# Sums of two pairs of node tiles per layer gathered by GpSimd with adding indirect DMAs, in a graph layer and expert kernel

## What is computed

```python
norm = dis[src] * dis[dst]                       # dis = 1/sqrt(degree), self loops included
for l in range(2):
    x_res = x
    h = x @ W[l]
    agg = segment_sum(norm[:, None] * h[src], dst) + b[l]
    x = relu(agg + x_res @ resW + resb)
...
h1 = relu(features @ expert_w1 + b1); h2 = relu(h1 @ expert_w2 + b2); out = h2 @ expert_w3 + b3
combined = sum over the two best experts of weight * out
```

## Time and profile before

| | us |
|---|---|
| three runs, median (lowest to highest) | 2029.84 (2025.51 to 2032.26) |
| the profiled execution, its own time | 2028.8 |
| its span in the trace | 2027.2 |

### The profile page before, as it was taken

One profiled execution on the slowest core, in us unless ns is written; L12 is line 12 of the kernel. 1 busy time (PEld: TensorE's weight loads), 2 busy tenths in 40 slices (PEclk: granted clock), 3 DMA queues, 4 the chain that ended last, 5 costly groups with the idle time before them and its releaser, 6 DMA issues. The chain is left out here.

```text
span 2027.2 us, 34554 instructions
## 1 busy us (share of the span) xinstructions
PE 1845.7 (91%) x11170; PEld 1128.0 (56%) x11170; DVE 1120.7 (55%) x2788; ACT 771.5 (38%) x1686; POOL 387.4 (19%) x403
## 2 busy tenths in 40 slices
PE   4448799999999999999959999999999988998886
PEld 3336555555555555555524445444454476886775
DVE  7246766666666666666504444444444566644443
ACT  2226755665566655665501222222222232221221
POOL 1680000000000000000000211111211133335664
PEclk8769899999999999999979999999999999998998
DMA  6255399998999972323364555444555556767783
GB/s 221 58 85 111 106 330 308 285 333 257 293 293 272 282 248 94 153 108 134 154 274 159 184 193 203 173 174 170 184 202 196 186 183 200 253 214 234 256 254 123
DMA packets 121920, 412.55 MB, mean 204 GB/s; under 512 B 14633, under 2 KB 75009, under 8 KB 115577
## 3 DMA queue, kind: packets, MB, share of 16 engines
q1 hardware_dynamic: 82936, 283.65, 40.2%
q0 software_dynamic: 37904, 124.85, 21.9%
q10 hardware_dynamic: 1008, 3.21, 0.4%
HBM read 201.60 MB, written 219.99 MB: 208 GB/s over the span
## 5 line engine op out<-in xcount | busy, mean ns | idle before, releaser
L1383 PE MATMUL bank<-parts,counts 128*128 128x512 f16 x2401 | 643.3, 378 | 0.0
L1383 PE MATMUL bank<-parts,counts_again 128*128 128x512 f16 x2401 | 540.3, 381 | 18.5 <-DMA counts_again<-counts_table 18.5
L1547 ACT ACTIVATE counts<-bank 128x392 f16<-128x392 f32 x800 | 395.1, 497 | 311.2 <-PE bank L1463 304.5
L1383 PEld LDWEIGHTS bank<-parts,counts_again 128*128 128x128 f16 x2401 | 234.1, 99 | 288.4 <-issue 17.0
L594 DVE TENSOR_TENSOR rows_lo<-pair_keys,iota_lo 128x2048 bf16<-128x2048 bf16 x200 | 244.9, 1225 | 239.4 <-PE bank L1463 239.3
L1463 PEld LDWEIGHTS bank<-rows_hi,rows_lo 128*128 128x128 bf16 x3200 | 227.6, 99 | 203.7 <-issue 27.1
L1463 PE MATMUL bank<-rows_hi,rows_lo 128*128 128x98 bf16 x3200 | 277.8, 210 | 11.3 <-DVE rows_hi L594 10.5
L1383 PEld LDWEIGHTS bank<-parts,counts 128*128 128x128 f16 x2401 | 192.5, 96 | 103.6 <-issue 1.1
L454 POOL DMA_INDIRECT first_rows<-route_rows,route_spot_i x49 | 47.9, 977 | 825.7 <-DVE tokens L445 817.7
L594 DVE TENSOR_TENSOR rows_hi<-pair_keys,iota_hi 128x1568 bf16<-128x1568 bf16 x200 | 193.5, 967 | 0.0
L2261 DVE TENSOR_SCALAR h_t<-bank,counts_again 128x256 f32<-128x256 f32 x120 | 57.7, 483 | 161.4 <-PE bank L2097 115.6
(11 more groups left out here) (259 smaller groups left out, 1843.1 us busy)
## 6 DMA issues: line engine op xcount, KB each, us to landing
counts_table<-counts SPq DMA_DIRECT2D x25, 3136.0 KB, 13.7
counts_again<-counts_table SPq DMA_DIRECT2D x24, 3136.0 KB, 11.4
counts_again<-expert_pack SPq DMA_DIRECT2D x60, 898.0 KB
first_rows<-zero_rows POOLq DMA_DIRECT2D x3, 10530.0 KB, 58.4
second_rows<-zero_rows POOLq DMA_DIRECT2D x3, 10449.0 KB, 70.2
res_tile<-res_table SPq DMA_DIRECT2D x98, 128.0 KB, 6.5
first_rows<-zero_rows POOLq DMA_DIRECT2D x1, 10270.0 KB, 61.8
second_rows<-zero_rows POOLq DMA_DIRECT2D x1, 10191.0 KB, 66.7
```

The lines of the kernel that those rows point to most:

```text
L1383: mm = nc.tensor.matmul(acc[:, 0:2 * dim], lhs, rhs, start=s == 0, stop=s == tiles)
L1547: nc.scalar.activation(counts[:, b, :, :].rearrange("p s (o n) -> p o s n", o=2)[:, :, :, q * QUAD:(q + 1) * QUAD], bank[4 + q % 4][:, 0:Q ...
```

## The change

1. **Gathered sums.** Pairs 18 and 20 (`GATHERED`) no longer have counts. A float32 copy of all messages is kept in DRAM for each layer (`message_table`). The sum of each of their four tiles is made by GpSimd: in round n an indirect DMA reads, for each of the 128 nodes of a tile, the message of its n-th edge's source and adds it (`compute_op=ALU.add`) to `gathered_sums`. Nodes have up to 56 edges (`RUN`), shorter lists point at rows of zeros. So there are 56 rounds of four DMAs (128 rows of 1 KB each), 224 in each layer. The two DMAs of a pair wait until that pair's round before has landed. In layer 0 the 56 rounds stand one behind the other in GpSimd's queue; in layer 1 there are 8 rounds first, and then 3 behind the scatters of each pair.
2. **PE, DVE, ACT** do 23 pairs in both layers. The work that follows a sum (transposes, products, routing) stays for all 49 tiles; for pairs 18 and 20 it is put beside the pair after. In layer 1 the order of the routing of the pairs 17 to 23 is written out by hand (`LATE_ROUTES`), with a third buffer and a second bank.
3. **Preparation.** GpSimd's 40 weight DMAs are gone from here. In their place GpSimd adds, for each tile, high half and rest to the float32 message (L904 of the new file; once more for the four gathered tiles, whose own message starts the sum, L903), SP stores these rows six tiles at a time (L846) and the stage ends only when they have landed. `rest` has four buffers instead of two; DVE waits for the addition of four tiles before. DVE works out the lists of sources (`sources`), for which GpSimd gathers four more windows (L914).
4. **Weights.** SP now issues the packing (`pack_weights`, 52 DMAs), at the start of layer 0, between its first load of residual rows and the store of the first counts. Twelve of them write zeros: one block of 256 rows at the start of each expert's region in both tables.
5. **No zero fill.** The eight fills of both tables are gone. An expert's last block no longer runs past the last row into zeros: it ends at the last row, begins earlier, and the rows already done are masked (`done_before`).
6. **Layer 0** also stores each tile's message in float32 for layer 1 (128 KB for each tile, on SP).

```diff
+    GATHERED = (18, 20)
+    RUN = 56
...
+        def gather_round(pool, l, n, own_ready=None):
+            for h in range(len(GATHERED)):
+                if n > 0:
+                    pool.wait_ge(gathered[h], 32 * (l * RUN + n))
+                elif own_ready is not None:
+                    pool.wait_ge(own_ready, 32)
+                pool.sem_inc(pool_link, 1)
+                for m in (2 * h, 2 * h + 1):
+                    pool.indirect_dma_start(gathered_sums[:, m, :], None, message_table[l], bass.IndirectOffsetOnAxis(ap=source_of[:, m, n:n + 1], axis=0),
+                                            compute_op=ALU.add).then_inc(gathered[h], 16)
...
     def store_next(self, eng, T, o):
         eng.wait_ge(self.res_out, T + 1)
+        eng.wait_ge(self.messages_ready, T + 1)
         eng.dma_start(self.res_table[self.l + 1][bass.ds(T * P, P), :], self.res_next[:, o, :]).then_inc(self.res_stored[o], 16)
+        eng.dma_start(self.message_table[self.l + 1][bass.ds(T * P, P), :], self.scaled[:, o, :]).then_inc(self.res_stored[o], 16)
...
                 for t in range(tiles):
                     pool.indirect_dma_start(windows[:, t, :], None, edge_list, bass.IndirectOffsetOnAxis(ap=start_i[:, t:t + 1], axis=1)).then_inc(fetched[t // BATCH], 16)
-                pool.dma_start(router_w1_sb[:, :, :], router_w1.rearrange("(k p) d -> p k d", p=P)).then_inc(first_w_loaded, 16)
...
+                    nc.gpsimd.tensor_tensor(room[n % 2][:, at, :], rest[:, t % 4, :], parts[:, t, 0:dim], ALU.add).then_inc(message_made, 1)
...
                     dve.wait_ge(high_ready, t + 1)
-                    if t >= 2:
-                        dve.wait_ge(middle_ready, t - 1)
+                    if t >= 4:
+                        dve.wait_ge(middle_ready, t - 3)
+                        dve.wait_ge(message_made, t - 3)
...
                     update.load(sp, 0, 0, 0)
+                    pack_weights(sp)
                     store_counts(0, 0)
                     pair(0, 0)
                     pair(1, 1)
-                    with sp.Fori(1, pairs // 2) as j:
+                    with sp.Fori(1, LATE // 2) as j:
...
                 @block.gpsimd
                 def _(pool):
-                    store_zeros(pool)
+                    for n in range(RUN):
+                        gather_round(pool, 0, n)
                     update.wait_stored(pool)
...
+        LATE_ROUTES = {19: ((17, ROUTE_AT), (18, (92, None, None, None))),
+                       21: ((18, (None, 6, 14, 34)), (19, (44, 52, 60, 92))),
+                       22: ((20, (4, 12, 20, 40)), (21, (50, 58, 66, 94))),
+                       23: ((22, ROUTE_AT),),
+                       24: ((23, ROUTE_AT[0:3] + (None,)),)}
+        FIRST_ROUNDS, ROUNDS = 8, 3
...
-                    pool.wait_ge(zeros_stored, ZEROS)
...
+                    for h, g in enumerate(GATHERED):
+                        pool.dma_start(gathered_sums[:, 2 * h:2 * h + 2, :], message_table[1][2 * g * P:2 * (g + 1) * P, :].rearrange("(t p) d -> p t d", p=P)).then_inc(own_back, 16)
+                    for n in range(FIRST_ROUNDS):
+                        gather_round(pool, 1, n, own_back)
+                    for p in range(LAST_PAIR - 1):
+                        router.scatter(pool, p, buffer_of(p), 2)
+                        for n in range(FIRST_ROUNDS + p * ROUNDS, min(FIRST_ROUNDS + (p + 1) * ROUNDS, RUN)):
+                            gather_round(pool, 1, n)
```

More of the change, by code:

```diff
@@ L494, in gnn_moe_kernel @@
     W_COLS = 3 * K2 * dim + 2 * K2 + dim
+    GATHERED = (18, 20)
+    BACK = 2 * len(GATHERED)
+    RUN = 56
+    LATE = GATHERED[0]
+    late_pairs = tuple(i for i in range(LATE, pairs) if i not in GATHERED)
     slots = 64
@@ L1526, in pair @@
+                            if there(first):
                                 if r == 5:
-                                    sums(i - 1, 0)
+                                    sums(n - 1, 0)
                                 if r == 7:
-                                    update.res_and_message(dve, i * 2 - 2, 0, i - 1)
-                    for i in range(4):
-                        pair(i, i % 2)
-                    with dve.Fori(2, pairs // 2) as j:
+                                    update.res_and_message(dve, first, 0, pair_at(n - 1))
@@ L1534, in _ @@
+                    for n in range(4):
+                        pair(n, n % 2)
+                    with dve.Fori(2, LATE // 2) as j:
                         pair(j * 2, 0)
                         pair(j * 2 + 1, 1)
-                    pair(pairs - 1, 0)
+                    for n in range(LATE, summed):
+                        pair(n, n % 2)
                     update.rest_of(dve, tiles - 3, 0)
                     for T in (tiles - 2, tiles - 1):
-                        sums(T // 2, T % 2)
+                        sums(nth(T // 2), T % 2)
@@ L1558, in pair @@
+                    def pair(n, j, b):
+                        if not isinstance(n, int) or n >= 2:
                             act.wait_ge(counts_stored[b], j * 16)
-                            act.wait_ge(update.sums_ready, 2 * i - 2)
+                            act.wait_ge(update.sums_ready, 2 * n - 2)
+                        ending, second, gathered_tiles, first = before_counts(n)
                         for q in range(quads):
-                            quad(q, i, b)
-                            if q == 0 and there(i * 2 - 4):
-                                update.middle_part(act, i * 2 - 4, 0)
@@ L1582, in pair @@
-                                if q == 28:
-                                    update.high_part(act, i * 2 - 2, 0, i - 1)
-                    for i in range(4):
-                        pair(i, i // 2, i % 2)
-                    with act.Fori(2, pairs // 2) as j:
+                                    update.turned_copy(act, first, 0)
+                                if q == (30 if gathered_tiles else 28):
+                                    update.high_part(act, first, 0, pair_at(n - 1))
+                    for n in range(4):
+                        pair(n, n // 2, n % 2)
@@ L1588, in _ @@
+                    with act.Fori(2, LATE // 2) as j:
                         pair(j * 2, j, 0)
                         pair(j * 2 + 1, j, 1)
-                    pair(pairs - 1, pairs // 2, 0)
+                    for n in range(LATE, summed):
+                        pair(n, n // 2, n % 2)
                     update.middle_part(act, tiles - 3, 0)
                     for T in (tiles - 2, tiles - 1):
-                        middle_sums(T // 2, T % 2)
+                        middle_sums(nth(T // 2), T % 2)
@@ L1843, in _ @@
                     work.begin_list(dve)
-                    by_pairs(dve, pair)
+                    by_summed(dve, pair, late)
                     def beside(b):
```

723 lines of the change are left out of this document (481 added, 242 removed).

## The result

The changed kernel takes 2183.43 us (median of 5 runs, 2176.84 to 2196.5); the kernel before, measured beside it, 2025.51 (5 runs, 2019.6 to 2032.26). The ratio is **1.0784 [1.0739, 1.0829]: slower by 158 us**. The prediction said 1971, and its range ended at 2100. The profiled execution took 2196.5 us, its span is 2195.0.

A forecast was written before the change was run, and what follows sets the result against it. PE was taken to bound both layers. Gain -98.4, preparation +3, layer 0 start +19, layer 1 start +4, late pairs +4, GpSimd's DMAs disturbing others +10: -58.4, so 1971 us; own range 1950 to 1995, holding range 1940 to 2100.

The forecast's parts named there:

- What bounds the kernel, and the gain: Both layers: PE is the limit; two pairs fewer save 55.2 us in layer 0 and 43.2 in layer 1, 98.4 together.
- Preparation: Stage before layer 0: +3 us (-6 to +12), from stores landing sooner against new DVE steps, additions and a last store.
- the term of -8: In the preparation, ACT's 8.07 us wait for the residual rows' store goes once GpSimd's weight DMAs are gone: -8 us.
- Start of layer 0: Layer 0, near 281 us: the packing ahead of the first counts store makes ACT and PE wait, +19 us (0 to +25).
- Start of layer 1: Start of layer 1: loads of counts share the DMA engines with the first 8 gather rounds, +4 us (0 to +8).
- Rival 1: Layer 0: adding DMAs without pauses make PE's updates late, costing 124 us; 2084 us in all, chance 0.34.
- the pauses that the prediction counted on: Gather rounds: an adding DMA lands after 4 to 5 us, over the 4.0 needed, leaving a short pause each round.
- Layer 1's sums in time: Layer 1: gathered sums ready before DVE needs them, no cost put; a round's issues 5.3 us, a landing 4 to 5.
- rival 2: Layer 1: gathered sums come late for DVE, 26 to 66 us, taken as 40; 2010 us in all, chance 0.11.
- the sign that the prediction named: Layer 1: DVE waiting for `gathered_sums` before pair 19 would show the forecast wrong; no size given.
- Layer 0 "safe" at 10.7 us a round: Layer 0: 19 x 31.44 / 56 leaves 10.7 us for each gather round, so its sums would not come late.
- Rival 3: Layer 1: GpSimd's issues wait for running DVE operations, 19 us late; 1989 us in all, chance 0.04.

The follow-up runs named there:

- the copies of layer 1: The changed kernel with layer 1's gathers copying instead of adding: 1916.41 us, 0.9772; where the kernel before takes 2022.51 us, 2117.28 us, 1.0464.
- 2025 groups: Groups of runs in which the unchanged kernel before, measured beside the others, takes some 2025 us; in the other groups it takes some 1961.
- the one-pair kernel: The changed kernel gathering only pair 20, in layer 1 by staged copies that DVE adds, packing spread: 1928.88 us, 0.982; in another group 2003.28 us, 0.9902.

## Why the prediction was wrong, step by step

- **What bounds the kernel, and the gain.** Right. Layer 1 without gathers is 42 us shorter for 43.2. In layer 0 PE is busy for 47.6 us less (777.01 to 729.40), not 55.2; around two waits at the layer's start the granted clock is 0.80 and 0.93 for 52 and 31 us, which would make the remaining matmuls longer; that this is the whole rest was not worked out. An unchanged pair takes what it took the earlier trace rows: (772.5 - 395.2) / 6 = 62.88 us for two.
```profile
L1652 DVEq FUSED_REGOPS  x7: 64/64/64, 395.2 to 772.5; - x7
```
- **Preparation** +3.2 for +3. The sum fits, and the term of -8 is seen: ACT no longer waits for the residual rows' store, but waits 12.7 us for DVE's `rest` where it waited 5.0. The other parts were not measured alone.
- **Start of layer 0** 19 us forecast at about 281, with the store of counts as its end; it was 22.3 us, ended at 309.06. Timeline of PE, and what ACT waited for:
```profile
309.06 0.49 PE L1595 MATMUL bank<-rows_hi,rows_lo 128*128 128x98 bf16 x4 [22.26 <-ACT counts L1698]
```
```profile
ACT counts L1698 <- DMA counts_table<-counts: 25.3, 1, 25.3
```
- **Start of layer 1** +13.8 for +4, half of it from a cause that the prediction did not have. At the border GpSimd's queue drains its DMAs before its block ends; lines of the change and of before:
```profile
L1583 POOLq DRAIN  x1: 6670/6670/6670, 1007.6 to 1007.6; - x1
```
```profile
L1451 POOLq DRAIN  x1: 143/143/143, 1026.9 to 1026.9; - x1
```
- **Rival 1** (chance 0.34) did not come: in layer 0 additions ran 1.85 us apart and more, with PE at 100.00 of 100. Its mechanism exists, as the copies of layer 1 show, but for DMAs 1.25 us apart and in the 2025 groups only. What kept it away may be the longer issue and not the pauses that the prediction counted on: in layer 1, 16 DMAs of the changed kernel follow each other without a pause (1392.00 to 1419.27), and nobody waits for "remote" there. As far as that is so, it was luck.
- **Layer 1's sums in time: the step that failed.** The forecast put nothing for GpSimd being too slow in layer 1; it had 5.3 us for the issues of a round and 4 to 5 for a landing. Measured: 4 x 1.85 = 7.4 for the issues, and landings of 13.2 us beside a load of counts and of 20.5 at the layer's start, where GpSimd waits until 1047.28 for the gather of 1026.75. The prediction's name for this is rival 2, with chance 0.11 and 40 us, at a landing of 6 or 7. The first 8 rounds took 93.6 us (1021.04 to 1114.61), 11.7 each where it had 7.3, and a pair 35.1 where it had 25.3. Put into its formula: 1021 + 93.6 + 16 x 35.1 = 1676, which is when GpSimd did end its gathers, 212 us past the 1464 that the prediction had as their deadline. Layer 1 took 212 us over the 546 without gathers. So the amount of GpSimd's work was counted rightly and its prices were not: they rested on the duration and landing of a plain gather, taken where the DMA engines were busy for 0.27 of the time (1820 to 1830), against 0.65 in the changed layer 1.
```profile
1026.75 1.54 POOL L630 DMA_INDIRECT gathered_sums<-message_table,source_of  x1 [0.31 <-issue]
...
1047.28 1.54 POOL L630 DMA_INDIRECT gathered_sums<-message_table,source_of  x1 [4.82 <-DMA gathered_sums<-message_table,source_of]
```
- **The way it reached PE was missing too.** Rival 2, and the sign that the prediction named, have DVE wait for `gathered_sums` before pair 19. That wait came, once and for 16.9 us. The other 208.9 us of DVE's waits are for the buffers of the scatters, which stand behind the gathers in GpSimd's queue, in 16 pairs; the prediction counted the scatters only as work of GpSimd and never as something that DVE waits for.
```profile
DVE layer_sum L142 <- DMA gathered_sums<-message_table,source_of: 16.9, 1, 16.9
```
- A sign stood in the formula itself: even at 6 us a pair needed 10.7 + 14.6 = 25.3 us of a GpSimd that has 23.3. A stage whose helper needs more than the period has no margin left to carry an unknown price; that should have weighed more than 0.11.
- **Layer 0 "safe" at 10.7 us a round** was used up: 56 rounds from 234.3 to 850.8 took 11.0 each, and DVE waited 8.48 us for the sums, of which 3.83 reached PE.
- **Rival 3** (GpSimd waits for DVE). Not seen in layer 1: copies take 0.94 us while DVE works for 248 of 500 us, and additions 1.55 whether a DVE operation runs at their start or not. In layer 0 it is there. Of 222 additions, 127 begin while a comparison L658 runs and take 2.18 us on average; 68 begin while DVE does nothing and take 1.55. Timelines of DVE and GpSimd:
```profile
406.41 0.97 DVE L658 TENSOR_TENSOR rows_hi<-pair_keys,iota_hi 128x1568 bf16<-128x1568 bf16 x1
```
```profile
406.63 2.17 POOL L630 DMA_INDIRECT gathered_sums<-message_table,source_of  x1 [0.30 <-issue]
409.11 1.55 POOL L630 DMA_INDIRECT gathered_sums<-message_table,source_of  x1 [0.30 <-issue]
```
The first of these ends 1.42 us after the comparison (407.38 to 408.80), and nearly all of the 127 do the same. It made the mean addition of layer 0 longer by 0.37 us (1917 ns), which had room there. Why operations of DVE hold issues up in layer 0 and not in layer 1, no run tells.

What stays open: why updates come late in some groups while GpSimd issues densely and in others not. And pauses among the window gathers together with the one-pair kernel were not tried; each alone gains 29 and 19 us in the 2025 group where both ran.

## What to carry to other kernels

Before moving work to GpSimd's DMAs, set the helper's own period (issues x measured cost, plus the landing that each chained round waits for) against the period of the stage; where it is close, price the landing beside the biggest load that shares the engines, not alone. A chain of additions into one buffer pays that landing once per round, and everything queued behind it on GpSimd pays too, and so does whoever waits for that: two sums in turn took 148 us off. Take half the work if all of it does not fit: one pair in place of two, with copies that DVE adds in layer 1 and the packing spread, turned +7.8% into -1.0 to -1.8%. Which of the three did how much was not taken apart.

## What the hardware showed that was not expected

- An adding indirect DMA of 128 rows of 1 KB occupies GpSimd for 1.54 us, a copy of the same rows for 0.94, each with 0.30 between. An addition that begins while DVE runs one of layer 0's comparisons ends 1.42 us after that comparison.
- The landing of an adding one is anything from under 5.6 us (1406.52 to 1412.08) to 13.2 beside a load of 3 MB, and 20.5 at the start of layer 1. The Trainium skill, "DMA: Bandwidth & Descriptors", section "Anatomy of one DMA", prices a GpSimd DMA of this size at some 2.0 us plus its bytes at 436 GB/s, 2.3 us as an estimate; the runs disagree, as soon as a large load stands on the same engines.
- At the end of layer 0, GpSimd's drain takes 6.67 us after 224 adding DMAs, the last of them 157 us before, and 6.75 after 112; it takes 0.14 in the kernel before, where only large direct DMAs stood there.
- The same kernel before takes 1961 us in some groups of runs and 2025 in others, and the larger part of the difference lies in 69 us of preparation, where GpSimd issues 49 gathers without a pause. A wait after every fifth is worth -1.5% in the latter and costs 0.9% in the former.
